# Depthwise 5x5 convolution as 32x32 TensorE tiles, and the routed values on GpSimd, in a hybrid routing-attention / transformer / mixture-of-experts kernel

## The reference, cut to what matters

```
q  = xw @ wq.T * gq + bq                 # xw: 256 windows of 2x2 pixels, 128 channels
kv = xw @ wkv.T * gkv + bkv              # 128 key and 128 value channels
_, r_idx = top_k(q_win * SCALE @ k_win.T, 4)          # 4 windows for each window
k_sel, v_sel = kv_pix[r_idx]                          # 16 keys and values for each window
attn = softmax(einsum('npmqc,npmkc->npmqk', q * SCALE, k_sel))    # 8 heads of 16 channels
out  = einsum('npmqk,npmkc->npmqc', attn, v_sel)      # the routed values
lepe = depthwise_conv(v_img, w_lepe 5x5, padding 2) + b_lepe
x = x + (out + lepe)
```

## Time and profile before

| | us |
|---|---|
| median of 3 runs | 2214.54 (2210.95 to 2215.18) |
| the profiled execution, its own time | 2220.89 |
| its span from first to last instruction | 2219.0 |
| TensorE busy | 1603.0 (72%) |
| VectorE busy | 1488.3 (67%) |
| GpSimd busy | 1143.7 (52%) |
| ScalarE busy | 928.6 (42%) |

### The profile page before, as it was taken

One profiled execution on the slowest core, in us unless ns is written; L12 is line 12 of the kernel. 1 busy time (PEld: TensorE's weight loads), 2 busy tenths in 40 slices (PEclk: granted clock), 3 DMA queues, 4 the chain that ended last, 5 costly groups with the idle time before them and its releaser, 6 DMA issues.

```text
span 2219.0 us, 39848 instructions
## 1 busy us (share of the span) xinstructions
PE 1603.0 (72%) x15168; PEld 1059.0 (48%) x15168; DVE 1488.3 (67%) x2572; ACT 928.6 (42%) x1273; POOL 1143.7 (52%) x582
## 2 busy tenths in 40 slices
PE   2004457886879767886878767897678868898897
PEld 1002235553556435553556545564456535564565
DVE  3794569757785668758686578857686577841554
ACT  0000127522674227631564216732375226642683
POOL 0994789145960689226880569406890459600000
PEclk9557769997899878998889979998799988888898
DMA  4201200030000200030000300021000300000000
GB/s 130 76 0 38 77 1 2 1 125 1 1 2 30 98 1 1 2 104 23 1 1 1 126 1 1 1 67 59 1 1 1 115 1 1 1 1 11 1 2 10
DMA packets 26168, 62.04 MB, mean 28 GB/s; under 512 B 4192, under 2 KB 13408, under 8 KB 25824
## 3 DMA queue, kind: packets, MB, share of 16 engines
q0 software_dynamic: 9216, 33.56, 4.4%
q1 hardware_dynamic: 16736, 25.60, 3.6%
HBM read 46.56 MB, written 12.58 MB: 27 GB/s over the span
## 4 chain that ended last, share of the span: by engine, by line
PE 29%; issue 25%; DVE 21%; POOL 10%; ACT 3%; DMA 2%; DVEq 1%; POOLq 0%; SPq 0%; ACTq 0%
POOL KV L1237 8%; PE psB L404 7%; PE psB L536 5%; DVE P L1048 5%; DVE Q L948 3%; PE psA L585 2%; POOL KVSEL L1224 2%; PE psB L520 2%; PE psB L554 2%; DVE STACKED L1095 2%; DVE PROD L941 2%; DMA window_table<-KV 2%; PE psB L501 2%; PE psB L513 1%; PE psB L517 1%
## 5 line engine op out<-in xcount | busy, mean ns | idle before, releaser
L1253 POOL TENSOR_TENSOR XLEPE<-XLEPE,KV 128x1024 f32<-128x1024 f32 x200 | 498.8, 2494 | 16.7
L1237 POOL TENSOR_TENSOR KV<-KVSEL,Q 128x1024 f32<-128x1024 f32 x112 | 306.9, 2763 | 154.9 <-DVE KVSEL L917 119.8
L536 PE MATMUL psB<-W,P 128*128 128x128 f32 x2048 | 308.0, 298 | 102.7 <-DVE NEGMAX L1048 95.8
L1048 DVE CUSTOM_DVE_ANT_0 P<-psB,W 128x1024 f32<-128x1024 f32 x256 | 312.0, 1219 | 74.4 <-PE psB L404 44.5
L729 ACT ACTIVATE P<-P,NEGMAX 128x1024 f32<-128x1024 f32 x256 | 293.0, 1144 | 114.6 <-DVE NEGMAX L1056 112.6
L1224 POOL DMA_INDIRECT KVSEL<-window_table,CHOSEN x64 | 60.8, 950 | 536.8 <-DMA window_table<-KV 491.2
L536 PEld LDWEIGHTS psB<-W,P 128*128 128x128 f32 x2048 | 250.4, 152 | 176.9 <-issue 128.8
L1250 POOL TENSOR_SCALAR KV<-V_PAD,W 128x1024 f32<-128x1024 f32 x200 | 273.8, 1369 | 72.3 <-POOL XLEPE L1253 39.8
L737 ACT ACTIVATE PT<-psB 128x1024 f32<-128x1024 f32 x256 | 260.3, 1017 | 56.0 <-PE psB L536 54.3
L404 PE MATMUL psB<-TN,W 128*128 128x512 f32 (+1 forms) x512 | 252.2, 627 | 12.2 <-DVEq L1098 9.5
L948 DVE TENSOR_REDUCE Q<-PROD 128x128 f32<-128x2048 f32 x64 | 240.5, 3757 | 0.3
(11 more groups left out here) (117 smaller groups left out, 2094.8 us busy)
## 6 DMA issues: line engine op xcount, KB each, us to landing
window_table<-KV SPq DMA_DIRECT2D x8, 1024.0 KB, 6.1
X<-x_by_window_dram SPq DMA_DIRECT2D x8, 512.0 KB, 5.3
XLEPE<-x_dram SPq DMA_DIRECT2D x8, 512.0 KB, 3.9
out_dram<-PT SPq DMA_DIRECT2D x8, 512.0 KB, 3.8
W<-packed_dram SPq DMA_DIRECT2D x1, 3714.5 KB, 11.5
KVSEL<-window_table,CHOSEN POOLq DMA_INDIRECT x64, 5.4
FC<-packed_dram SPq DMA_DIRECT2D x8, 64.0 KB, 2.3
PROD<-gains_dram SPq DMA_DIRECT2D x1, 256.0 KB, 12.3
```

The costliest lines, as they stand in the source:

```text
L536: mm = pe.transpose(ps[:, t * 128:(t + 1) * 128], P[:, i % P_BUFFERS, t * 128:(t + 1) * 128], ident)
L1048: dve.tensor_tensor_reduce(P[:, b, :], ps[:], w("band", at, at + TOK), 1.0, -3.0e38, ALU.mult, ALU.max, NEGMAX[:, b, 0:1]).then_inc(free, 1)
L1237: pool.tensor_tensor(PRODUCTS[i % 2].rearrange("p (k c) -> p k c", c=C), KVSEL[:, t, keys, 0:C], Q[:, t, q, :].unsqueeze(1).broadcast_to([ ...
L1253: pool.tensor_tensor(acc, acc, product, ALU.add).then_inc(lepe_done, 1)
```

## The change

The 25 taps leave GpSimd. TensorE takes them as matmuls with 32x32 diagonal weight matrices, on the image's values in V_PAD, in two passes `a` of 64 channels each: for every tap, four blocks `c` of eight rows of the image and two blocks `b` of 32 channels, 8 matmuls of 32x32 by 256 columns; a 26th group of eight adds x from XLEPE by the identity. That is 52 groups of 8 matmuls an image. The result lies in psA with image blocks on the partitions; ScalarE copies it to a buffer of P (`lepe_copy`), and 16 DMAs of 32x256 on SyncE's queue put it into XLEPE with channels on the partitions. The groups are woven into TensorE's order by `LEPE_BEFORE`, at seven places from the last expert to the values of stage C.

GpSimd takes the routed values instead: for each tile and pixel the product of 2048 elements, then four additions of 1024, 512, 256 and 128 elements, and for each tile the scaling. VectorE's `value_steps` are gone but for tile 1 of image 0. `EARLY_STEPS` is 8, and the list of VectorE's steps is shorter. The gathers of both tiles now stand ahead of the first key product. `sums` waits for the scaled values of the image before, since they are worked out in PROD. The scores `u = 2` wait for the 16 DMAs, since the copy lies in that buffer of P. The ring of psA is counted by a new class, `ImageRing`.

```diff
+LEPE_PASSES = 2
+LEPE_GROUPS = [(a, tap) for a in range(LEPE_PASSES) for tap in range(TAPS5 + 1)]
+LEPE_BEFORE = {("dw", 0, 0): 12, ("dw", 1, 0): 8, "fc2": 10, ("centred", 0, 0): 6, ("var", 0, 0): 5, ("rstd", 0, 0): 6, "v": 5}
+LEPE_DMAS = 16
-LINKS_A2 = 30
-EARLY_STEPS = 6
-MLP_STEPS = 20
-WINDOW_STEPS_AT = [3, 5, 8, 11, 14, 17, 19, 22, 25, 28]
+LINKS_A2 = 14
+EARLY_STEPS = 8
+LATE_STEPS = 2
...
+            def spread_lepe(m):
+                sp.wait_ge(lepe_copied, 2 * (m + 1))
+                for a in range(LEPE_PASSES):
+                    for b in range(2):
+                        r, at = 2 * a + b, HALF * b + 256 * a
+                        for c in range(4):
+                            sp.dma_start(XLEPE[32 * r:32 * r + 32, 256 * c:256 * c + 256],
+                                         LEPE_OUT[32 * c:32 * c + 32, at:at + 256]).then_inc(lepe_in, 16)
...
+            def lepe_taps(m, groups):
+                for a, tap in groups:
+                    if (a, tap) == LEPE_GROUPS[0]:
+                        pe.wait_ge(diag_ready, 8)
+                        pe.wait_ge(v_ready, PX * (m + 1))
+                        for b in range(2):
+                            pe.wait_ge(a_free[b], RING_A.turn(("lepe", b), m))
+                    if (a, tap) == (1, 0):
+                        pe.wait_ge(lepe_half_done, 2 * (m + 1))
+                    if (a, tap) == (0, TAPS5):
+                        pe.wait_ge(raster_in, 16 * (m + 1))
+                    dy, dx = divmod(tap, 5)
+                    for c in range(4):
+                        for b in range(2):
+                            rows = slice(64 * a + 32 * b, 64 * a + 32 * b + 32)
+                            if tap < TAPS5:
+                                late, k = divmod(tap, early_taps)
+                                weights = LEPE_DIAG[late][rows, k, :]
+                                values = V_PAD[rows, 8 * c + dy:8 * c + dy + 8, dx:dx + SIDE]
+                            else:
+                                weights, values = ident[rows, rows], XLEPE[rows, 256 * c:256 * c + 256]
+                            mm = pe.matmul(psA[b][32 * c:32 * c + 32, 256 * a:256 * a + 256], weights, values,
+                                           start=tap == 0, stop=tap == TAPS5)
...
+            def lepe_copy(m):
+                for b in range(2):
+                    act.wait_ge(a_ready[b], RING_A.turn(("lepe", b), m))
+                    act.activation(LEPE_OUT[:, HALF * b:HALF * b + HALF], psA[b][:], ACT.Copy).then_inc(lepe_copied, 1)
...
                 load_table(ACT.Exp, 1, n)
+                if second is not None:
+                    lepe_copy(second)
+                    a_exp(1, second)
...
                     dve.wait_ge(x_in, 16 * (m + 1))
+                    if not (isinstance(m, int) and m == 0):
+                        dve.wait_ge(attended_ready, WTILES * m)
...
-                woven = [step for pair in zip(value_steps(0), key_steps(1)) for step in pair]
-                return key_steps(0) + softmax_steps(0) + woven + softmax_steps(1) + value_steps(1)
+                second_keys = key_steps(1)
+                steps = key_steps(0) + [lambda: less_maximum(0)] + second_keys[:4] + [lambda: sum_keys(0)]
+                steps += second_keys[4:] + [lambda: less_maximum(1), lambda: sum_keys(1)]
+                return steps + (value_steps(1) if alone else [])
...
-                    run(later, {4: 1, 5: 1, 6: 2, 7: 2}.get(e, 0))
+                    run(later, {5: 1, 6: 1, 7: EARLY_STEPS - 2}.get(e, 0))
...
-            def taps(m):
-                for tap in range(TAPS5):
-                    pool.tensor_scalar(product, V_PAD[:, dy:dy + SIDE, dx:dx + SIDE], col("lepe_w", tap), 0.0,
-                                       ALU.mult, ALU.add).then_inc(tap_ready, 1)
-                    pool.tensor_tensor(acc, acc, product, ALU.add).then_inc(lepe_done, 1)
+            def values(m, t):
+                pool.wait_ge(e_ready, WTILES * m + t + 1)
+                for q in range(PX):
+                    pool.tensor_tensor(PROD[:].rearrange("p (k h c) -> p k h c", k=KEYS, h=HEADS_A),
+                                       KVSEL[:, t, :, C:2 * C].rearrange("p k (h c) -> p k h c", h=HEADS_A),
+                                       S[t][:, q].unsqueeze(3).broadcast_to([128, KEYS, HEADS_A, CH_A]),
+                                       ALU.mult).then_inc(value_step, 1)
+                    for keys in (8, 4, 2, 1):
+                        into = PROD[:, 0:keys * C] if keys > 1 else Q[:, t, q, :]
+                        pool.tensor_tensor(into, PROD[:, 0:keys * C], PROD[:, keys * C:2 * keys * C], ALU.add
+                                           ).then_inc(value_step, 1)
+                        pool.wait_ge(value_step, done)
+                pool.wait_ge(sums_ready, WTILES * m + t + 1)
...
             def window_stage(m):
+                for t in range(WTILES):
+                    gathers(m, t)
+                for t in range(WTILES):
+                    for i in range(2 * PX):
+                        key_product(m, t, i)
+                for t in range(WTILES):
+                    values(m, t)
...
             for t in range(WTILES):
                 gathers(0, t)
-            taps(0)
+            for i in range(2 * PX):
+                key_product(0, 0, i)
+            values(0, 0)
             window_stage(1)
```

More of the change, by code:

```diff
@@ L95, in turn, with __init__, slot @@
         return n * self.uses[s] + k + 1
[L98 to L105, removed]
-    def turn(self, name, m):
[L109 to L121, removed]
+class ImageRing:
+    def __init__(self, first, body, ahead, slots):
+        self.body, self.ahead = body, ahead
+        self.place = {name: i % slots for i, name in enumerate(body)}
+        self.first = first + [(name, ahead(name) - 1) for name in body if ahead(name) > 0]
+        self.emitted = self.first + [(name, n + ahead(name)) for n in range(IMAGES) for name in body
+                                     if n + ahead(name) < IMAGES]
+    def slot(self, name):
+        return self.place[name]
+    def turn(self, name, m):
+        s = self.place[name]
+        if isinstance(m, int):
+            before = self.emitted[:self.emitted.index((name, m)) + 1]
+            return sum(self.place[other] == s for other, _ in before)
+        on_slot = [other for other in self.body if self.place[other] == s]
+        first = sum(self.place[other] == s for other, _ in self.first)
+        return (m - self.ahead(name)) * len(on_slot) + first + on_slot.index(name) + 1
+ROUTED = ["windows", "logits"] + [("qkv", t, p) for t in range(WTILES) for p in range(PX)] + [("v", 0), ("v", 1)]
+LEPE = [("lepe", b) for b in range(2)]
+RING_A = ImageRing([(name, 0) for name in ROUTED],
+                   LEPE + [("pv", t) for t in range(TT)] + [("attended", t) for t in range(WTILES)] + ROUTED,
+                   lambda name: 2 if name in ROUTED else int(name in LEPE or name[0] == "attended"), 2)
 class EarlyRing(Ring):
@@ L601, in stages_b_to_d @@
             def stages_b_to_d(n, second, first):
+                groups = list(LEPE_GROUPS)
                 for name in ORDER_B:
+                    if second is not None:
+                        count = LEPE_BEFORE.get(name, 0)
+                        lepe_taps(second, groups[:count])
+                        groups = groups[count:]
                     if name not in RING_B.early:
@@ L649, in a_values @@
             def a_values(m):
-                if not (isinstance(m, int) and m == 0):
-                    act.wait_ge(lepe_done, TAPS5 * m)
                 for hy in range(2):
@@ L769, in stages_b_to_d @@
                     turned(u, n)
-                    if second is not None and u == WINDOW_STEPS_AT[STEPS_TO_SOFTMAX - EARLY_STEPS - MLP_STEPS] - 1:
-                        a_exp(1, second)
                     if u == PROJECTED + 3:
@@ L806, in _ @@
             a_values(0)
+            lepe_copy(0)
             a_exp(0, 0)
@@ L1045, in scale_scores @@
                     b = u % P_BUFFERS
+                    if u == 2 and second is not None:
+                        dve.wait_ge(lepe_in, 16 * LEPE_DMAS * (second + 1))
                     at = TOK - 128 - 128 * (u // HEADS_C)
```

122 lines of the change are left out of this document (68 added, 54 removed).

## The result

The changed kernel takes 1954.4 us (median of 4 runs, 1951.16 to 1960.88) against 2212.7 us of the kernel before beside it: a ratio of 0.883, 95% interval 0.880 to 0.886. The prediction was 1980 in 1930 to 2080. The profiled execution took 1960.9 us, its span 1959.1 (before: 2219.0), and the mean granted clock rose from 0.852 to 0.918.

What follows compares the result with a forecast made beforehand. VectorE's steps were taken to lengthen an attention stretch TensorE could do in about 100 us. Start -36, attention -140, convolution -44, router to convolution -21 and copy +7 give -234: about 1980 us, range 1930 to 2080.

Steps and rivals of the forecast that it cites:

- Attention stretch: From stage C's values to the next router on TensorE: 131.2 us falls to 111, -140 us for seven images.
- plus 5.3 for the projections: Attention stretch: 5.3 us added to the last image's 106.0 for projections, from 131.2 - 125.9.
- The -1.5 for the clock: Attention stretch: 1.5 us off because the last image's values ran at a cold clock and now follow tap matmuls.
- GpSimd's beside work costs VectorE little: Attention stretch: with GpSimd busy 82 us there, VectorE's own instructions explain the difference.
- Rival 3: The attention stretch doesn't shorten, another engine taking VectorE's place; TensorE would keep it at 125: 2080 us. Chance 0.05.
- Convolution stretch: From the 3x3 convolution to stage C's values on TensorE: 59.5 us, 6.3 less an image, -44 for seven.
- The +4 for emptied pipelines: Convolution stretch: 4 us added for the pipeline running empty where tap groups end before larger matmuls, and between passes.
- Router to convolution: From the router to the 3x3 convolution on TensorE: -3.5 us an image, -21 for six.
- The start: Image 0: values shared by GpSimd and VectorE, the residual starting at 155 instead of 190.89, -36 us (-25 to -42).
- GpSimd's ring: GpSimd's work per image: loses 25 taps, gains 85 us for values; 188 us against a period of 226, slack 38.
- Rival 2: GpSimd's ring decides, if values take over 1.45 times 85 us: 2000 us upward. Chance 0.04 below the old time, 0.04 above.
- Rival 1: Tap matmuls go slower than 30 ns: 2030 us at 39 ns, 2135 at 57 ns. Chance 0.22.

Runs made afterwards that it cites:

- second measurement: The changed kernel run again unchanged, as reference for the first group of experiments: 1961.5 us, ratio 0.888 to the kernel before.
- The kernel without value pairs: The kernel before, with VectorE's eight product-and-sum pairs of the routed values left out from image 1 on, taps still on GpSimd: 1950.5 us.
- the written-out kernel: The changed kernel with TensorE's loop over six images written out, nothing else changed: 1930.1 us, ratio 0.877 to the kernel before.
- the doubled values: The changed kernel with every product and addition of the routed values done twice on GpSimd: 2153.0 us.
- The thinned kernel: The changed kernel with 24 of the 25 taps of each pass left out, leaving 64 of 832 records an image: 1841.3 us.

## Why the prediction was right, and which terms were off

The mechanism was right in its main part, and the total was off by 25 us, for errors of 45 us on one side and 20 on the other.

**Attention stretch.** Predicted 111 us, measured 107.2, and the 1 us for the copy isn't seen. The term that was too large is "plus 5.3 for the projections". I had read it off the difference between an image with projections and one without, but both rows come from a stretch that VectorE ended, so 5.3 us is what VectorE's share of that work cost there. With VectorE free the difference between images 5 and 6 is 107.2 - 103.6 = 3.6 us. The rest is in the base: the last image's stretch, in which VectorE was never late, takes 106.0 us in the kernel after and 102.1 in its second measurement and five of the other kernels. The windows of it, the first of the kernel after and the second of its second measurement, have the same VectorE and ScalarE, and a granted clock of 0.93 and 0.98:

```profile
1802.77:1908.76 105.99, 98.07 (x984) 67.76 (x984) 64.40 (x136) 81.17 (x114) 0.00 (x0) 0.93 0.01 1
```
```profile
1809.49:1911.62 102.13, 93.73 (x984) 63.81 (x984) 64.41 (x136) 80.90 (x114) 0.00 (x0) 0.98 0.01 1
```

The -1.5 for the clock should have been -4; with both, the sum is 106.6. The kernel without value pairs reaches the same 107 with the taps on GpSimd: taking away the pairs is enough. That GpSimd's beside work costs VectorE little was wrong, though the sum didn't use it: without it the same instructions take VectorE 4.7 us less (95.9 against 100.6). Rival 3 is out.

**Convolution stretch.** Predicted 59.5, measured 57.6 to 61.4. The sum came out right from terms that weren't. The tap records take 27.3 ns instead of 30 where the clock is up. The +4 for emptied pipelines is under 1 us, as the written-out kernel's tap blocks show. In their place stands the half clock, which I had credited as gone (-8): it came back behind the branch and behind the variance's one-column matmuls. The statement of the Trainium skill (TensorEngine Tiling (Array Packing), key properties of the tiling modes), that a change of tiling mode drains TensorE, is not refuted, but at 0.16 us a block it is a quarter of the 0.69 us by which I had priced it, and the 18 us more aren't there. "TensorE is what is late next" was right: VectorE waits 12.62 us for fc2 (predicted some 8), and thinning the taps shortens the stretch to 48.7.

**Router to convolution.** Predicted 55.5, measured 55.6 to 61.1 in the kernel after and 54.0 to 55.6 with the loop written out. The step "the taps fill until 999" left out the branch at the end of TensorE's loop body. Before, it lay inside a wait for VectorE of 8.15 us, where it didn't show. With that wait gone it is itself the gap, and the clock mostly falls behind it. This is a wait that takes the place of the one removed, and a rival that I should have listed. It is the term on the slow side: 20 us of a forecast 21 didn't come here, and the loop written out takes 31 us off in all, part of it behind this stretch.

**The start.** Up to the 3x3 convolution of image 0 it is -38.0 us, 2 more than predicted, and from there to its values -19.8 instead of -6.3. This second part is most of the start's miss: I had given image 0 the steady image's gain. Before, TensorE stood ahead of fc2 and of centred there:

```profile
262.61 9.26 PE L510 MATMUL psB<-PT,FC 64*128 64x512 f32 x32 [21.75 <-ACTq L684]
295.20 3.77 PE L513 MATMUL psB<-XR,W 128*128 128x512 f32 x4 [23.33 <-DVEq L1078]
```

In the kernel after there is no wait ahead of that fc2, and 2.70 us ahead of centred. The first part hides two errors. The residual was predicted at 155 and starts at 144.51: -46 instead of -36. But the convolution follows it 32 us later instead of 24, now that 192 tap records, 5.5 us, stand between. The values of image 0 took GpSimd 50.4 us, not 59. Two rows of VectorE and three of GpSimd there:

```profile
119.27 4.76 DVE L1019 TENSOR_TENSOR KV<-KVSEL 128x2048 f32<-128x2048 f32 x1
144.51 2.40 DVE L1060 SCALAR_TENSOR_TENSOR XLEPE<-psA,W,XLEPE 128x128 f32<-128x128 f32 x8 [2.75 <-PE psA L472]
...
104.91 5.55 POOL L1322 TENSOR_TENSOR PROD<-KVSEL,S 128x2048 f32<-128x2048 f32 x1 [0.18 <-POOL Q L1330]
118.21 3.68 POOL L1322 TENSOR_TENSOR PROD<-KVSEL,S 128x2048 f32<-128x2048 f32 x1 [0.18 <-POOL Q L1330]
142.15 1.06 POOL L1336 TENSOR_TENSOR Q<-Q,SUMS 128x512 f32<-128x512 f32 x1
```

VectorE's product at 119.27 takes 4.76 us beside a GpSimd product that ends at 121.9, against 2.29 alone: the turns are there, as priced, but a GpSimd product takes 3.68 alone, not 4.7.

**GpSimd's ring.** Predicted 85 us for the values, measured 74.3 (893.7 to 968.0). `sums` comes 51 us behind their end, where I had 38; the doubled values give about 50. Rival 2 is out for this kernel, and shown to be real at twice the work. At twice the work I had put 2330; it is 2153, as the pass is 74 us and not 85.

**What costs nothing.** The 16 DMAs take 10.05 us on SyncE's queue, as estimated, and no scores wait for them.

**Rival 1** is half true. Cold records take 56 ns, in steady images in the stretches behind the branch and the variance. By the rival's own measure, busy time by records, the whole of L500 comes near its 39 ns: 148.6 us for the group shown first, 91.5 for the one below and 13.4 for the additions of x make 253.5 us for 6656 records, 38 ns each, image 0's hidden ones with them. The stretch stayed at its 59.5 us because the +4 for emptied pipelines was hardly needed. The thinned kernel puts the taps' price at 113 to 120 us.

```profile
L500 PE MATMUL psA<-V_PAD,LEPE_DIAG 32*32 32x256 f32 x2304 | 91.5, 450 | 1.4 <-issue 1.4
```

What stays open: what decides when the clock falls in the layer norm, and for how long. In the kernel after it falls in each of images 1 to 6, while the variance runs or up to 2.5 us behind it, and stays down for 4 to 14 us (fc2 to values varies from 24.7 to 27.9 us); with all taps ahead of fc2 it doesn't fall in three of the six.

## What to carry to other kernels

When a wait is taken away, look for what had been hidden inside it on the waiting engine itself: here a loop's way back of 2.4 us, behind which the clock was mostly cold. Read the price of beside work only in stretches that the engine in question doesn't end; a difference between two stretches bound by VectorE says nothing of one bound by TensorE. When a change of order is priced by its sign and size alone, a wrong cause can pass: look at the stretches. One half of a change can be worth nothing alone: work that moves into a wait is free only up to the instruction that waits, and what stands behind it is paid in full.

## What the hardware showed that I had not expected

- A branch at the end of TensorE's loop body showed as 2.41 us without work and a second gap of 0.66 us, and the granted clock was 0.50 for about 10 us behind it. So it was behind nine of the ten such branches in the two traces of the kernel after; with the loop written out it took 31 us less in all.
- The granted clock also fell to 0.50 with no wait ahead, behind 16 fp32 records of one column.
- A GpSimd product of 128x2048 fp32 with a factor broadcast along the innermost dimension took 3.68 us, less than two products of 1024 (2.4 each).
- An fp32 record of a 32x32 tile with 256 columns, on 8 parts, took 27.3 ns at full clock and 56 at half, hardly less than one of 512 columns on 16 parts at full clock (29.4).
